# Layer 3 channel attention: scores made a second time turned, maxima split into bf16 words on GpSimd

## The reference, cut to what matters

```
qh = q.reshape(b * 8, 16, 256); kh, vh = the same of the context
qk = einsum('bdm,bdn->bmn', qh, kh) / sqrt(16)       # 256 x 256 scores a head
sm = softmax(qk, axis=-1)
ret = einsum('bmn,bcn->bcm', sm, vh)                  # back to 128 x 256
x = x + ret                                           # q was layernorm(x)
```

## Time and profile before

| | us |
|---|---|
| median of 3 runs (lowest, highest) | 1596.16 (1592.63, 1598.41) |
| span of the profiled execution, first to last instruction | 1562.7 |
| what lies around the span, median less span | 33.5 |
| the stage of layer 3's attention, from its first load to the next stage's first | 190.5 |

### The profile page before, as it was taken

The page is one execution under the profiler, slowest core; times in us unless marked ns, Lnnn a source line. Parts: engine busy times, 40 slices in busy tenths (PEclk is TensorE's granted clock), DMA queues, the critical chain, the costliest instruction groups (busy, mean ns, idle before and its releaser), DMA issues. The chain is left out here.

```text
span 1562.7 us, 29997 instructions
## 1 busy us (share of the span) xinstructions
PE 1345.7 (86%) x8381; PEld 881.4 (56%) x8382; DVE 1023.1 (65%) x2409; ACT 829.3 (53%) x2371; POOL 627.0 (40%) x660
## 2 busy tenths in 40 slices
PE   5899996798689888899989999978996999978993
PEld 3555553466444353576555666554773666656992
DVE  5898897477469847333655888875334888864224
ACT  3767764687420045331107888843442888835561
POOL 3112420899477232673001111112545665214661
PEclk9999998899799878999997999998996999997997
DMA  5131000500000061695301000241552111411225
GB/s 188 48 100 36 17 16 28 191 0 1 27 27 0 1 193 42 186 308 181 94 14 31 24 23 23 69 147 41 146 143 81 49 54 30 176 58 58 87 87 168
DMA packets 96448, 124.82 MB, mean 80 GB/s; under 512 B 11117, under 2 KB 76464, under 8 KB 96112
## 3 DMA queue, kind: packets, MB, share of 16 engines
q1 hardware_dynamic: 85760, 95.80, 19.4%
q0 software_dynamic: 10608, 28.07, 6.3%
HBM read 91.31 MB, written 33.43 MB: 80 GB/s over the span
## 5 line engine op out<-in xcount | busy, mean ns | idle before, releaser
L717 ACT ACTIVATE l0a_prob<-l0a_ps_s,l0a_neg_max 128x128 f32<-128x128 f32 x512 | 137.9, 398 | 73.2 <-DVE l0a_neg_max L559 67.6
L717 ACT ACTIVATE l2a_prob<-l2a_ps_s,l2a_neg_max 128x128 f32<-128x128 f32 x512 | 138.7, 402 | 26.0 <-DVE l2a_neg_max L559 21.3
L1160 ACT ACTIVATE l3a_prob<-l3a_ps_s,l3a_neg_max 128x256 f32<-128x256 f32 x256 | 104.5, 483 | 31.9 <-DVE l3a_neg_max L1074 30.4
L219 POOL TENSOR_TENSOR ln_rstd<-ln_var_eps,minus_half 128x4 f32<-128x4 f32 (+1 forms) x14 | 23.0, 1651 | 244.6 <-POOLq L183 213.4
L559 DVE TENSOR_REDUCE l2a_neg_max<-l2a_ps_s 128x4 f32<-128x512 f32 x128 | 85.7, 684 | 20.2 <-PE l2a_ps_s L815 19.3
L502 POOL TENSOR_TENSOR l2a_k_head<-l2a_kT,head_of_row 128x512 f32<-128x512 f32 x32 | 33.1, 1054 | 157.5 <-DMA l2a_kT<-k_rows 157.5
L568 DVE COPY l0a_probT<-l0a_ps_t 128x512 f32<-128x512 f32 x128 | 84.7, 683 | 14.9 <-PE l0a_ps_t L827 14.8
L559 DVE TENSOR_REDUCE l0a_neg_max<-l0a_ps_s 128x4 f32<-128x512 f32 x128 | 85.5, 684 | 10.2 <-PE l0a_ps_s L815 9.6
L1074 DVE TENSOR_REDUCE l3a_neg_max<-l3a_ps_s 128x2 f32<-128x512 f32 x128 | 84.0, 680 | 10.7 <-PE l3a_ps_s L1210 10.5
L1832 PE MATMUL l1a_ps_y<-l1a_kv,l1a_tap 128*128 128x512 f32 x192 | 85.6, 609 | 3.7 <-POOL l1a_kv L1804 3.7
L502 POOL TENSOR_TENSOR l0a_k_head<-l0a_kT,head_of_row 128x512 f32<-128x512 f32 x32 | 32.6, 1039 | 139.8 <-DMA l0a_kT<-k_rows 139.8
(11 more groups left out here) (489 smaller groups left out, 3534.2 us busy)
## 6 DMA issues: line engine op xcount, KB each, us to landing
expert_results<-zeros SPq DMA_DIRECT2D x1, 8320.0 KB, 26.3
l1f_got<-expert_results SPq DMA_DIRECT2D x16, 512.0 KB, 3.9
expert_results<-l2f_y_sb SPq DMA_DIRECT2D x47, 128.0 KB, 1.8
l1f_w_gu<-in_l1f_w_gu SPq DMA_DIRECT2D x16, 352.0 KB, 6.2
l2f_w_gu_all<-in_l2f_w_gu SPq DMA_DIRECT2D x1, 4096.0 KB, 14.0
l3f_w_gu_all<-in_l3f_w_gu SPq DMA_DIRECT2D x1, 4096.0 KB, 13.6
l3f_got<-expert_results SPq DMA_DIRECT2D x16, 256.0 KB, 5.3
l1f_w_d<-in_l1f_w_d SPq DMA_DIRECT2D x16, 176.0 KB
```

The costliest lines, as they stand in the source:

```text
L717: last = act.activation(prob[4 * c + j][:, r * P:r * P + P], ps_s[j][:, r * P:r * P + P], ACT.Exp, bias=neg_max[:, j, r:r + 1])
L1160: last = act.activation(prob[4 * c + j][:, m * D:m * D + D], ps_s[j][:, m * D:m * D + D], ACT.Exp, bias=neg_max[:, j, m:m + 1])
```

## The change

The scores are no longer transposed after the exponential. A first pass makes them as before, for the maxima alone. The maxima are then taken off by the matrix unit in a second pass that makes the scores with keys on the partitions:

- DVE writes the negated maximum of each head into word 0 of a block of 32 words a head (`shifts`, zero elsewhere). POOL (`split`) takes the upper bf16 half off word 0 into word 1, and the upper half of that off into word 2, so that the upper halves of the three words add up to the f32 maximum. It does so for each half of a tile: two small subtractions with a drain between. The splits stand in POOL's queue ahead of `combine` and ahead of `spread`, one more ahead of the first gathers.
- PE turns the words (`turn_shift`: two bf16 transposes a half), ACT copies them (`copy_shift`), PE writes their sum to all partitions of a PSUM buffer with a matmul of ones (`take_shift`: bf16, 32 contraction rows, 512 columns) and adds the turned scores (`score_again`: two f32 matmuls a head, `start=False`).
- ACT takes the exponential once a head, 512 wide and without a bias, straight into the layout that `weigh_values` reads. `turn_prob`, `copy_probT` and `probT` go.
- The second pass of tile b-1 runs in batch b of PE's loop, pair of heads by pair of heads, with the first pass of tile b; buffers and loops go by threes (`over_threes`, 18 batches). Score buffers: three for the first pass, three for the second. SP's context loads are written out and wait for `e_put`.

The core of the diff; first POOL's part, then ACT's `batch`, then PE's `scores` (a pair of heads of tile b and of `before`, tile b - 1) and PE's `batch`. The conditions for the first and last tiles are left out here:

```diff
+            def split(b, c):
+                word, top = shift_word[c], shift_top[c]
+                pool.wait_ge(max_done, b * CH + 4 * c + 4)
+                pool.tensor_tensor(word[:, :, :, 1], word[:, :, :, 0], top[:, :, :, 0], ALU.subtract)
+                pool.drain()
+                pool.tensor_tensor(word[:, :, :, 2], word[:, :, :, 1], top[:, :, :, 1], ALU.subtract).then_inc(split_done, 1)
             find_rstd(0, READY)
+            spread(0)
+            spread(1)
+            split(0, 0)
             for t in range(RING, RING + READY):
                 gather(t)
             for b in range(2, B):
                 t = b + READY - 2
+                split(b - 2, 1)
                 if t < B:
                     combine(t)
                 if t + RING < B:
                     pool.drain()
                     gather(t + RING)
+                split(b - 1, 0)
+                spread(b)
...
+            def batch(b, r, turn):
+                    exps(b - 1, (r - 1) % 3, 0, 0)
+                    exps(b - 1, (r - 1) % 3, 0, 1)
+                    copy_o(b - 2, 1)
+                    exps(b - 1, (r - 1) % 3, 0, 2)
+                    exps(b - 1, (r - 1) % 3, 0, 3)
+                    copy_shift(b - 1, 1)
+                    exps(b - 1, (r - 1) % 3, 1, 0)
+                    exps(b - 1, (r - 1) % 3, 1, 1)
+                    copy_o(b - 1, 0)
+                    exps(b - 1, (r - 1) % 3, 1, 2)
+                    exps(b - 1, (r - 1) % 3, 1, 3)
+                    values(b + 1, (r + 1) % 3, turn + (r == 2))
+                    copy_shift(b, 0)
...
+            def scores(b, r, turn, s):
+                    for j in first:
+                        score(b, r, c, j, 0)
+                    for at in ats:
+                        take_shift(*before, at)
+                    for at in ats:
+                        score_again(*before, at, 0)
+                    for j in first:
+                        score(b, r, c, j, 1)
+                    for at in ats:
+                        score_again(*before, at, 1)
...
+            def batch(b, r, turn):
+                scores(b, r, turn, 0)
+                    weigh_values(b - 2, r2, 1)
+                scores(b, r, turn, 1)
+                    turn_shift(b - 1, 1)
+                    turn_o(b - 2, 1)
+                scores(b, r, turn, 2)
+                    weigh_values(b - 1, r1, 0)
+                    turn_attn(b - 2, r2)
+                scores(b, r, turn, 3)
+                    turn_o(b - 1, 0)
+                    turn_shift(b, 0)
```

More of the change, by code:

```diff
@@ L935, in _, with over_threes, within @@
             project_out(B - 1)
+def over_threes(eng, body):
+    for b in range(3):
+        body(b, b, 0)
+    with eng.Fori(1, 4) as i:
+        for r in range(3):
+            body(i * 3 + r, r, i)
+    for b in range(12, B + 2):
+        body(b, b % 3, b // 3)
+def within(b, lo, hi):
+    return not isinstance(b, int) or lo <= b < hi
 def channel_attention(core, name):
@@ L965, in channel_attention @@
[L965 to L972, removed]
@@ L1116, in batch @@
-            def batch(b, u):
-                look = after(b, READY - 2) and ahead(b, 2)
+                dve.tensor_tensor(core.xt(b), core.xt(b), ps_out, ALU.add).then_inc(x_done, 1)
+            def batch(b, r, turn):
+                scored = within(b, 0, B)
+                done = within(b, 2, B + 2)
+                look = within(b, READY - 2, B - 2)
+                if done:
+                    weigh(b - 2, (r - 2) % 3, 0)
+                if not within(b, 0, B + 1):
+                    finish_rows(dve, core, 0, B - 1)
+                if scored:
+                    find_max(b, r, 0, 0)
+                    find_max(b, r, 0, 1)
@@ L1173, in copy_o @@
                     act.wait_ge(r_put, b * 2 + c - 1)
-                act.activation(o_sb[c][:, :], ps_o[:, :], ACT.Copy).then_inc(o_done, 1)
-            def batch(b, u):
-                for c in range(2):
-                    before = (b, 0) if c else (b - 1, 1)
-                    exps(b, c, 0)
-                    exps(b, c, 1)
-                    if c or after(b, 1):
-                        copy_probT(*before, 0)
-                    exps(b, c, 2)
-                    exps(b, c, 3)
-                    if c or after(b, 1):
-                        copy_probT(*before, 2)
-                    if after(b, 1):
-                        copy_o(b - 1, c)
-                    if c == 1 and ahead(b, 1):
-                        values(b + 1, 1 - u)
@@ L1200, in _ @@
+            act.wait_ge(const_done, 11)
+            values(0, 0, 0)
+            over_threes(act, batch)
         @block.tensor
         def _(pe):
[L1202 to L1213 removed]
@@ L1226, in weigh_values, with score @@
-            def weigh_values(b, c, u):
-                pe.wait_ge(t_done_a, b * 4 + 2 * c + 2)
-                pe.wait_ge(t_done_v, b * 4 + 2 * c + 2)
+            def score(b, r, c, j, m):
+                n = b * CH + 4 * c + j
+                rows = slice(32 * j, 32 * j + 32)
+                if m == 0 and (c or j == 3 or after(b, 1)):
+                    pe.wait_ge(max_done, n - 2)
+                mm = pe.matmul(ps_m[(r * CH + 4 * c + j) % 3][:, m * D:m * D + D], q_head[r][rows, c, m * P:m * P + P],
+                               ctx[r][rows, :], start=True, stop=True)
+                if m:
+                    mm.then_inc(s_put, 1)
@@ L1287 @@
+            over_threes(pe, batch)
 MAGIC = 1.5 * 2.0 ** 23
```

325 lines of the change are left out of this document (158 added, 167 removed).

## The result

The changed kernel takes 1619.39 us (median of 4, 1612.81 to 1628.76), the kernel before 1595.35 (median of 4): ratio 1.0157, 95% interval 1.0122 to 1.0191. The forecast was 1606 us, in a range up to 1618. The change is slower, as forecast, but by 24.0 us where 10.2 were expected.

The account below looks back on a forecast made before the run. PE was taken to bound the kernel at 10.75 us a tile, POOL second at 9.96. Start and gather tiles lose 11.0, later tiles win 0.8: + 10.2 on 1596.2 gives 1606 us, range 1592 to 1618.

Parts of the forecast that it names:

- The start: Up to tile 2: an extra memset and a split waiting for maxima ahead of the first gathers, 4.2 us lost.
- 1219.49 + 5.6 + 1.5: Old end of spread(2), plus first gather 5.6 us later, plus 1.5 for scaling and second subtractions behind the gathers.
- T2: Forecast time at which spread(2) ends on POOL and PE starts tile 2: 1227.1, 4.2 us later than PE before.
- POOL's tile with gathers, 11.6: POOL's work per gather tile: 9.96 plus 0.63 and 0.94 for two splits, 11.6 us with waits, ends 11.2 and 12.3.
- So POOL sets it: 11.6: From tile 2 to tile 10 POOL sets the pace, 11.6 us against 10.75, DVE's last maxima 1.5 us early.
- Rivals 3 and 4: Clock share 0.83: 1617 us, chance 0.12; DVE 2 us late with maxima so POOL's split waits: 1615 us, chance 0.12.
- 9.3 + 1.6 < 11.6: In gather tiles, PE's chain ending at 9.3 us plus 1.6 for a slow clock still fits within POOL's 11.6.
- T: Zero mark of the walk through a gather tile: the end of POOL's spread(b), where PE starts batch b.
- The ring from tile 10 on: Without gathers, PE and ACT set the pace from one copy_shift(b, 0) to the next: 10.1 us, ends 8.0 and 10.8.
- the term 0.22: Chosen time of the bf16 matmul in PE's pair-of-heads block of 1.06 us; ends 0.2 and 0.4.
- Rival 1: ACT's copies hide, gather-less tiles run at PE's 8.0 us and gather tiles at 11.2: 1590 us, chance 0.13.
- Rival 2: The 2.0 us behind the gathers aren't theirs, split's drain doesn't wait, gather tiles near 10.4: 1595 us, chance 0.08.

## Why the prediction came out too low

*What bounds the kernel before*: right. PE at 10.75, POOL at 9.96 with a drain behind the gathers; replacing the drains in the kernel before changed neither PE's pace nor, beyond its interval, the time.

*The start*: 32.2 forecast and 32.4 measured to q_head(2), in part by luck. The terms named (1219.49 + 5.6 + 1.5) add up to 1226.6; T2 = 1227.1 holds 0.5 that no term accounts for. The first gather came 13.1 behind the first memset, forecast 12.4, and this 0.7 filled the gap. PE took tile 2 another 0.9 later, at 1242.34; the forecast had it take q_head at once.

*POOL's tile with gathers, 11.6*: right where undisturbed, 11.3 to 11.4. The two subtractions cost 0.2 each and the second one's drain took over pow's cover, as walked through. What the drains cost, with all that follows from them, is shown by their replacement: 14.7 us less of stage.

*The step that failed is "So POOL sets it: 11.6"*, with no wait for maxima and the clock at 1.00. Eight such tiles took 98.2 and not 92.8: + 5.4. Four of them were long (14.35, 11.68, 13.19 and 13.50, the others 11.30 to 11.40). Rivals 3 and 4 were each priced alone: the clock as harmless in these tiles (9.3 + 1.6 < 11.6), the wait for maxima as DVE's doing. Here they are one mechanism. In the tile walked through above, PE has been idle for 2 us, the clock falls for some microseconds, and the last maxima come 13.3 behind T. Their split, at T + 11.4, had 1.1 us to spare at the full clock and now waits 2.1, and POOL, the bound, with it.

Three such waits (1.75, 1.83, 2.07) make 5.65. The drain ended 3.24 in place of 2.0 behind the gather in tile 3, and 2.30 in tile 4, where maxima that came late for the first subtraction have a part in it: 1.5. With eight tiles of 11.35 (90.8, 2.0 less than the forecast's 92.8) that is 98.0 of the 98.2. That filling PE's idle time brought the clock to 1.00 and took 4.8 us off the stage shows the clock's part. The first of the three waits stands apart: it stays with the filling (1.54), since tile 1 was made at half clock.

Two things stay open. Why the drain is longer in some tiles, and when the clock falls: PE had been idle for 1.81, 1.87 and 1.86 us ahead of three tiles in which it held, for 2.67, 1.95 and 1.53 ahead of three in which it fell, and for two pieces of 0.5 and 0.4 ahead of the fall in the kernel without splits.

By the Trainium skill (TensorE: Matmul & The Clock Gate, Part 1) the rate is the throttled one unless the engine was active of late; the runs agree in part (0.77 to 0.91 in some stretches with PE idle ahead of tiles, 1.00 in others with as much of it, 1.00 from 1230 to 1390 with the idle time filled).

*The ring from tile 10 on*: right as a mechanism, both stalls where forecast and both removed by reordering (10.47, 10.0, 9.7), but too small. I took 1.06 for two of the four blocks, and a block is 1.20; the term 0.22 for the bf16 matmul should have been 0.36, inside its ends. That is 0.28 of the 0.37 a tile. From tile 10 to the end: 79.2 for 75.2, + 4.0. Of this 1.9 is batch 10, counted to PE's second pass of the next batch at 1352.00: 12.4 for 10.5, begun at half clock again (0.83 between 1340 and 1350, a weighing of 1.94). The next four at 10.47 give 1.5, batch 15 and the tail 0.3 each.

0.2 + 5.4 + 4.0 = 9.6 is the whole miss in the stage. The stage alone, 19.7 more, would have given 1616 us. Of the 24.0 us that were timed it leaves 4.3, and I have no cause for them. They are of the size of what moves by itself: in the other timed kernels the change of the whole differs from that of the stage by - 3.9 to + 1.9 us, and in the nine traces at the slower level the stage begins anywhere from 1201.9 to 1209.0, though nothing ahead of it was edited.

*Rival 1* gave PE's own work as 8.0 a tile. The orders tried went down to 9.7 and no further; whether another one reaches 8.0 was not tried. *Rival 2*, that the 2.0 us were not the gathers', is refuted: with a drain the second subtraction waits 1.98, with a wait for its own instruction 0.30.

## What to carry to other kernels

Ahead of moving small work to an engine that looks half idle, read one tile of its timeline: a drain behind gathers isn't counted as busy, and what now comes behind it loses its cover. Where one instruction's result is all that is needed, wait for that instruction's semaphore. And price the clock and the waits together: an engine that keeps PE waiting for 2 us a tile may get its own inputs late in return, and with 1.1 us to spare that was enough here. Last, take the profile and the times that are to be added up from the same chip.

## What the runs showed of the hardware

- In most tiles a drain on POOL ends 1.9 to 2.1 us after the record of the last gather ahead of it, with 0.2, 0.6 or 1.0 to 1.2 us of work between them. It is not counted as busy. It can be longer, and I have no cause: 3.24 and 3.23 for tile 3 in two executions of the changed kernel (1249.45 to 1252.69 in the first), 2.3 to 2.6 in the early tiles of the kernel with the filling, and with the splits on DVE 2.25 to 2.47 in five later tiles and 2.99 for tile 2. So it isn't the splits on POOL that make it longer. A wait for POOL's own semaphore in the same place takes 0.30 from start to start, against 0.35 with a drain where no gather stands ahead. The Trainium skill (GPSIMD Engine Reference, 2.1 Instruction dispatch) says that an instruction's completion gates whoever waits on its semaphore and recommends that wait between dependent instructions; the runs agree and add the price of the alternative.
- The kernel before takes 1560 us on one chip and 1595 to 1599 on others, with this stage at 190.0 on the first and, with waits in place of drains, at 190.2 on one of the others. Behind the stage the span has 177.8 us left in the first trace of before, 177.6 in its second, 177.2 with splits on DVE on that chip; on the others 197.0 with the change and 199.8 for the kernel before with waits. The kernel with the filling has 190.5 in its slowest execution, on the first chip, so the chip is not all of it. What causes the difference was not looked for.
